# Moving the second and third part of the count transposes behind the first gather in the attention rows of a graph kernel

## The reference

```python
h = (x @ W).reshape(n, HEADS, C)                 # HEADS 4, C 32
e = leaky_relu(a_s[src] + a_d[dst], 0.2)         # one number per edge and head
p = exp(e - m[dst])                              # m: maximum over a node's edges
alpha = p / (segment_sum(p, dst) + 1e-16)
out = segment_sum(h[src] * alpha[:, :, None], dst) + gat_bias + x @ skip_W + skip_b
```

## Time and profile before

| | |
|---|---|
| median of three runs | 2859.01 us |
| the profiled execution's own time | 2859.01 us |
| its span in the profile | 2857.3 us |
| outside the span | 1.7 us |
| PE busy over the span | 2394.9 us (84%) |
| DVE busy | 2074.7 us (73%) |
| ACT busy | 1724.1 us (60%) |
| POOL busy | 485.8 us (17%) |
| part of `gat_rows` with its 13 super tiles | about 1129 to 2040 us of the span |

### The profile page before, as it was taken

One profiled execution on the slowest core, in us unless ns is written; L12 is line 12 of the kernel. 1 busy time (PEld: TensorE's weight loads), 2 busy tenths in 40 slices (PEclk: granted clock), 3 DMA queues, 4 the chain that ended last, 5 costly groups with the idle time before them and its releaser, 6 DMA issues. The chain is left out here.

```text
span 2857.3 us, 62252 instructions
## 1 busy us (share of the span) xinstructions
PE 2394.9 (84%) x16954; PEld 1632.8 (57%) x16955; DVE 2074.7 (73%) x3472; ACT 1724.1 (60%) x4122; POOL 485.8 (17%) x825
## 2 busy tenths in 40 slices
PE   1898989899988967888888888888749999869795
PEld 1444444454444545666666666666528888735453
DVE  6776777777772023999999999998558887566075
ACT  1898989999993015777777777776336666410101
POOL 0444444444441000000000000000000000011010
PEclk7999999999999988999999999999869999979897
DMA  1222322222226811222222222222123333067193
GB/s 40 95 106 94 111 94 105 100 108 102 100 106 265 306 57 49 95 95 94 94 94 94 94 94 94 94 94 72 53 94 121 132 115 115 3 269 328 56 426 122
DMA packets 132234, 341.18 MB, mean 119 GB/s; under 512 B 13957, under 2 KB 114936, under 8 KB 115704
## 3 DMA queue, kind: packets, MB, share of 16 engines
q1 hardware_dynamic: 131960, 338.62, 31.9%
HBM read 212.41 MB, written 126.18 MB: 118 GB/s over the span
## 5 line engine op out<-in xcount | busy, mean ns | idle before, releaser
L434 PE MATMUL ps_build<-OH,KEY 128*128 128x400 bf16 x4108 | 736.7, 339 | 82.6 <-ACT KEY L391 52.7
L391 ACT ACTIVATE KEY<-KEY,cols 128x128 bf16<-128x128 bf16 x2054 | 621.9, 398 | 100.4 <-DVE KEY L362 99.4
L434 PEld LDWEIGHTS ps_build<-OH,KEY 128*128 128x128 bf16 x4108 | 399.4, 99 | 420.2 <-issue 80.8
L1082 ACT ACTIVATE exponentials<-gr_ps,att_cols 128x256 f32<-128x256 f32 (+1 forms) x1300 | 496.2, 490 | 202.3 <-PE gr_ps L972 200.2
L362 DVE TENSOR_SCALAR KEY<-iota_key,key_base,cols 128x128 bf16<-128x128 int16 x1027 | 390.4, 412 | 217.8 <-PE ps_build L434 191.4
L409 POOL TENSOR_TENSOR KEY<-KEY,cols 128x256 bf16<-128x256 bf16 (+1 forms) x627 | 374.9, 599 | 500.0 <-DVE KEY L362 500.0
L972 PE MATMUL gr_ps<-ident,gr_r 128*128 128x128 f32 x2500 | 382.6, 292 | 65.7 <-DVE gr_r L1190 63.6
L1003 PE MATMUL gr_ps<-exponentials,heads 128*33 128x128 f32 x5000 | 364.8, 277 | 14.7 <-DVE exponentials L1197 14.7
L972 PEld LDWEIGHTS gr_ps<-ident,gr_r 128*128 128x128 f32 x2500 | 284.1, 147 | 149.7 <-issue 128.3
L1197 DVE SCALAR_TENSOR_TENSOR exponentials<-exponentials,gr_count_t 128x3072 f32<-128x3072 f32 (+1 forms) x104 | 349.4, 3360 | 22.4 <-ACT exponentials L1082 18.3
L1163 DVE CUSTOM_DVE_ANT_0 gr_unread<-gr_src_rows,gr_closed 128x3125 bf16<-128x3125 f32 (+1 forms) x100 | 344.2, 3442 | 15.0 <-ACT gr_closed L1075 14.4
(11 more groups left out here) (273 smaller groups left out, 1984.2 us busy)
## 6 DMA issues: line engine op xcount, KB each, us to landing
adjacency<-stage SPq DMA_DIRECT2D x200, 400.0 KB, 2.5
sage_ring<-count_by_source SPq DMA_DIRECT2D x50, 1600.0 KB, 9.2
agg_gcn_ring<-adjacency SPq DMA_DIRECT2D x25, 1600.0 KB, 8.2
gr_count<-adjacency SPq DMA_DIRECT2D x25, 1600.0 KB, 7.6
ar_counts<-adjacency SPq DMA_DIRECT2D x25, 1600.0 KB, 6.7
count_by_source<-gr_count_t SPq DMA_DIRECT2D x12, 3200.0 KB, 18.7
fg_node<-gat_node_sums SPq DMA_DIRECT2D x1, 1650.0 KB, 6.3
count_by_source<-gr_count_t SPq DMA_DIRECT2D x1, 1600.0 KB, 7.1
```

The costliest lines, as they stand in the source:

```text
L391: last = act.activation(KEY[:, slot + j, v, :], KEY[:, slot + j, 0, :], ACT.Copy, scale=k.cols[:, 1 + v, bass.ds(c + j, 1)])
L434: last = pe.matmul(ps[:, 2 * (s % 2) + (v > 0), 0:SL], KEY[:, slot + j, v, :], OH[:, slot + j, :], start=slot == s % 2 * (BODY + 1) and j ...
L1082: last = act.activation(e[:, s, 0:w], ps[:, i % RINGS, c:c + w], ACT.Exp, bias=cols[:, h, s:s + 1])
```

## The change

The two functions for part 1 and part 2 are one function now, and it is called after `join` and `gather_first` instead of before them. Nothing else is different; every wait stays at its instruction.

```diff
             def other_counts(g):
                 pe.wait_ge(raised, g * (HEADS * PIECES) + PIECES)
                 turn_counts(g, 1)
-
-            def last_counts(g):
                 pe.wait_ge(taken_n, g * 5 + (width(g) + 1))
                 turn_counts(g, 2)
@@
                     if h == HEADS - 1 and not is_super(g, LAST):
                         first_counts(g + 1)
+                    if before:
+                        join(g0, h0)
+                    gather_first(g, h)
                     if h == 0:
                         other_counts(g)
-                    if before:
-                        join(g0, h0)
-                    if h == 0:
-                        last_counts(g)
-                    gather_first(g, h)
```

## The result

The changed kernel took 2891.13 us (median of 4, 2888.77 to 2893.41), the kernel before 2859.06 us (median of 4 here). The ratio is 1.0112, with a 95% interval of 1.0095 to 1.013: 32 us slower, against 34.3 forecast. The profiled execution has a span of 2888.6 us, 31.3 more than before.

The account below looks back on a forecast made before the run. DVE, busy 98% of super tiles 1 to 11, was taken to bound the kernel. Stalls of 31.1 us there plus 1.6 each for the first and last super tile, 34.3, on 2859.0 gave 2893.3 us, range 2883 to 2900.

Parts of the forecast that it names:

- the main term: Super tiles 1 to 11: DVE stalls 2.83 us in each for the late counts, 31.1 us in all.
- the two end terms: Extra time in super tile 0 and in the single-tile last super tile, +1.6 us each.
- The counts are just in time: Head 0's third take on ACT ends so that DVE's `weigh_rest` has its counts only 0.43 us before starting.
- Join 0.05 behind the drain, gather 0.37 behind the join, 2.74 for the gather: Head 0 on PE: with join and gather going first, the counts start at 1506.57 instead of 1503.31, 3.26 us later.
- Super tile 0: No join here; DVE starts 1.62 us later with a half-clock gather of 5.48 us, or 1.12 earlier at full clock.
- The last super tile: Single tile without slack: counts 3.27 us later, +1.6 taken; ends 0 if PE and ACT catch up, 3.3 for the whole delay.
- I charge nothing: PE's new head 1 gaps, some 1.2 and 0.8 us, may halve its clock, but were said to cost no time.
- Hidden: Rival: counts are needed later than read, or the edit doesn't delay them; no change, 2858 to 2860 us; chance 0.03.
- faster: Rival: the earlier gather lets head 1 start sooner, saving at most 1.4 us per super tile, 2843.5 us; chance 0.02.
- Absorbed in part: Rival: the stall eats DVE's 1.4 us of idle time in each super tile, giving 2878 us; chance 0.07.
- The clock rival: PE's clock falls in head 0, gather and counts run at 1.2 GHz: 5.2 us per super tile, 2950 us; chance 0.05.
- The transfers cost nothing: ACT's `keep`, SP's stores and load run 3.26 us later, masks 2.83 late with 0.4 slack left; costed at nothing.

Follow-up runs that it names:

- experiments 2: Kernel before, with the join and the first 6 of the gather's 12 source blocks ahead of head 0's counts: 2874.91 us, ratio 1.0066.
- experiment 6: Kernel before, PE order unchanged, with an unread 128x3200 copy added on ACT between drain and first take in head 0: 2867.55 against 2857.36 us, ratio 1.0034.
- experiment 3: Changed kernel, with one DVE row maximum of head 1 put ahead of `weigh_rest`: 2867.09 us, ratio 1.0039 to the kernel before.
- experiment 1: Kernel before, with only the join ahead of head 0's counts and the gather still behind them: 2855.34 against 2855.22 us, ratio 1.0001.
- experiment 5: Kernel before, with only the last 2 count transposes behind head 0's gather, the others still ahead of the join: 2875.47 against 2857.36 us, ratio 1.0064.
- experiment 7: Kernel before, with `level`'s last two DVE steps given to POOL as three in heads 1 and 3, beside a moved `weigh_first`: 2870.06 against 2857.36 us.

## Why the prediction was right

The forecast was 2893.3 us in a range of 2883 to 2900, slower with a chance of 0.95. The measured 2891.13 is 2.2 below it. The mechanism held, and the main term is right to 2%; that the sum of the two end terms is right too is luck, as shown below. By its own steps:

- *DVE sets the pace, and a wait goes into the time in full.* Right: the period grew by 2.77 us for a stall of 2.76, and experiments 2 and 6 show the same at other sizes (1.47 for 1.38 of recorded wait, 0.68 for 0.60; the recorded wait leaves out the overlap of 0.08).
- *The counts are just in time, with 0.43 us of slack.* Right in kind. The measured stall is 2.76 instead of 2.83. Inside the loop DVE starts 0.03 us after the end of the take (1520.26 + 0.39 = 1520.65, then 1520.68), not the 0.11 read from super tile 0, so the slack is about 0.50. The 0.11 holds outside the loop, in super tile 0 of both kernels.
- *Join 0.05 behind the drain, gather 0.37 behind the join, 2.74 for the gather: 3.26 later.* Measured 3.27.
- *Eleven super tiles, 31.1 us.* Measured 30.56, from DVE's `gr_r` of super tile 1 to that of the last.
- *Super tile 0, +1.6, with -1.1 as the other end.* Mis-sized: from DVE's `gr_r` of head 1 on, it grew by 0.53 (56.04 against 55.51 us). The gather ran partly at half speed, 4.48 us by the row below, where a row at full speed lasts 2.81 and the forecast's slow case was twice 2.74; the counts behind it took their usual 2.84.

```profile
1140.74 4.48 PE L1001 MATMUL gr_ps<-exponentials,heads 128*33 128x128 f32 x48 [2.22 <-DVE exponentials L1193]
1145.15 2.84 PE L981 MATMUL gr_ps<-ident,gr_count 128*128 128x128 f32 x24
```

- *The last super tile, +1.6, up to 3.3.* Mis-sized the other way: 2.65 (41.04 against 38.39 us between the first and last `gr_r`). DVE's wait grew as forecast, from 2.41 to 5.68 us. But behind it the first 12 transposes of head 1 took 2.79 us instead of 1.53:

```profile
2030.99 0.33 PE L981 MATMUL gr_ps<-ident,gr_count 128*128 128x128 f32 x1 [1.60 <-ACT gr_count_t L1091]
2031.84 2.79 PE L972 MATMUL gr_ps<-ident,gr_r 128*128 128x128 f32 x12 [0.52 <-ACT gr_count_t L1095]
```

That is half speed: the granted clock from 2031.80 to 2034.60 was 0.50. The two gaps of 1.60 and 0.52 us don't explain it by themselves: experiment 3 has the same two gaps in its last super tile, and the 12 transposes behind them took 1.50 us there. Why the clock fell in the one and not in the other is open. "I charge nothing" for PE's clock was right in the loop, where head 1's transposes still took 2.84, and wrong by about a microsecond here. The two end terms were forecast at 1.6 each and measure 0.53 and 2.65: their sum, 3.18 against 3.2, is right because one was a microsecond too high and the other a microsecond too low.

- *Where the rest is.* From DVE's second `gr_r` of the layer to its last, the time grew by 33.7 us (908.53 against 874.79), against 34.3 forecast. The span grew by 31.3 only, since the part ahead of that point was 2.4 us shorter in the second profile. The programs are the same for nearly all of it, so this is variation from run to run. The medians' difference of 32 us can't be split in this way.
- *The rivals.* "Hidden" and "faster" fall with the result. "Absorbed in part" falls with the periods: DVE's other gaps are unchanged. The clock rival in the loop falls too: the counts took 2.84 us there.
- *The transfers cost nothing.* Not tested by itself. The mask of head 1 ran in one piece behind the drain in super tile 5, and DVE has no wait for it in the loop.

Experiment 3 adds a check of one more step. The prediction worked out that `weigh_first` of head 1 wouldn't wait for the twelve exponentials, with 1.7 us of room (1516.5 against 1518.18), because DVE's own stall gives them time. In the changed kernel it doesn't wait. With the stall of 2.76 us covered, that room is gone, and a wait of 1.05 us appears.

## What to carry to other kernels

On a stretch where one engine is busy 98% of the time, look for its instructions that start with no idle time ahead of them, and subtract the end of what they need: that slack, not the length of the work you move, tells what a delay will cost. Beyond the slack every tenth of a microsecond is paid in full and in every round; below it nothing is, as the 0.38 us of experiment 1. This was measured in one kernel, in the loop; in the single tile at its end PE and ACT share the pace, and a delay there follows no such line: takes 1.2 us late went with a last super tile 0.5 us shorter in experiment 5, and takes 1.3 us late with one 2.6 us longer in experiment 6. The last and smallest piece of a set is the one that counts: two transposes moved alone cost 18 us, 24 moved at another place about nothing in the loop.

## What the runs showed of the hardware that was not expected

A POOL instruction on 128x4 elements with operands in SBUF took 3.27 us beside a DVE instruction with two SBUF inputs, and 0.20 with DVE idle (experiment 7). The last super tile of that run has a second size: a POOL instruction on 128x2 elements took 1.68 us beside a DVE instruction of the same kind of 1.76 us, and ended 0.05 us after it.

The Trainium skill, page "SBUF — State Buffer", section "SBUF: two separate sides", says that DVE and GpSimd (POOL) share a pair of ports, and that whichever starts first holds the pair for its whole instruction, where a DVE instruction has two inputs in SBUF and the GpSimd one reads SBUF. The trace agrees, with POOL ending 0.06 and 0.05 us after DVE. The same POOL instruction beside a DVE instruction with one input was not run.
